# A six-stage transformer kernel on one core: the second attention's tables loaded a layer ahead, the last layer's first routing moved into the attention's last tile, and the attention's loop written out

## The reference

```
x = x + 0.5 * _L0_ffn_ref(_layernorm(x), ...)    # 4 experts, top 1, 128 -> 512 -> 128, gelu
x = x + _L0_attn_ref(_layernorm(x), ...)
x = x + 0.5 * _L0_ffn_ref(_layernorm(x), ...)
x = x + 0.5 * _L1_ffn_ref(_layernorm(x), ...)    # 32 experts of width 64, top 4
x = x + _L1_attn_ref(_layernorm(x), ...)         # 16 heads of 8, RoPE, softmax over 512 keys
x = x + 0.5 * _L1_ffn_ref(_layernorm(x), ...)
```

```
sel_logits = einsum('nd,ed->ne', xt, expert_sel); gates = sigmoid(sel_logits)
sel_val, sel_idx = top_k(gates, 4)               # gate_full: 0 outside the four
scores = relu(einsum('nd,edf->nef', xt, keys)) * gate_full[:, :, None]
out = einsum('nef,efv->nv', scores, values)

q, k, v = split(x @ w_qkv);  q, k = rope(q), rope(k)
attn = softmax(q k^T * 8 ** -0.5);  out = (attn v) @ w_proj + b_proj
```

## Time and profile before

| | us |
|---|---|
| median of three runs | 2547.51 |
| lowest, highest | 2541.93, 2551.03 |
| the profiled execution | 2552.19 |
| its span (first to last instruction) | 2550.4 |
| PE busy | 2252.5 (88%) |
| DVE busy | 1999.4 (78%) |
| ACT busy | 1298.6 (51%) |
| POOL busy | 962.2 (38%) |
| chain that ended last: PE, issue, DVE, DMA, ACT | 59%, 12%, 11%, 7%, 6% |

### The profile page before, as it was taken

The page is one execution under the profiler, slowest core; times in us unless marked ns, Lnnn a source line. Parts: engine busy times, 40 slices in busy tenths (PEclk is TensorE's granted clock), DMA queues, the critical chain, the costliest instruction groups (busy, mean ns, idle before and its releaser), DMA issues.

```text
span 2550.4 us, 39117 instructions
## 1 busy us (share of the span) xinstructions
PE 2252.5 (88%) x11234; PEld 1572.7 (62%) x11234; DVE 1999.4 (78%) x4669; ACT 1298.6 (51%) x1907; POOL 962.2 (38%) x868
## 2 busy tenths in 40 slices
PE   4399476749949999986999999999999998999999
PEld 3377355537737777764555555555555555777777
DVE  6588577748848999975888888888888885888887
ACT  1088232218824444442666666666666665444444
POOL 6600566420047777762122111112111202565654
PEclk9999655659969999996999999999999999999999
DMA  7243111024348888871111211111111113889886
GB/s 176 74 155 128 42 31 35 22 95 133 112 104 182 172 186 171 185 166 51 59 59 63 69 62 55 61 55 58 58 54 59 54 54 84 181 174 187 174 186 152
DMA packets 141318, 266.47 MB, mean 104 GB/s; under 512 B 19347, under 2 KB 22422, under 8 KB 140950
## 3 DMA queue, kind: packets, MB, share of 16 engines
q1 hardware_dynamic: 132790, 247.99, 39.7%
q0 software_dynamic: 8416, 17.25, 2.6%
HBM read 213.26 MB, written 54.31 MB: 105 GB/s over the span
## 4 chain that ended last, share of the span: by engine, by line
PE 59%; issue 12%; DVE 11%; DMA 7%; ACT 6%; SPq 3%; POOL 1%; POOLq 0%; DVEq 0%; ACTq 0%
PE ps L1960 10%; PE ps L1984 9%; PE ps L1971 8%; PE ps L1679 7%; PE ps L1681 7%; PE ps L1680 7%; DMA gate_rows<-gates_dram 4%; DVE m L1369 2%; ACT g L854 2%; PE ps L1693 1%; ACT g_hi L827 1%; PE ps L1686 1%; PE ps L1706 1%; DVE g_lo L1051 1%; DVE xnT_hl L1051 1%
## 5 line engine op out<-in xcount | busy, mean ns | idle before, releaser
L1533 DVE TENSOR_REDUCE shift<-ps 128x1 fp32r<-128x512 f32 x1024 | 664.2, 685 | 157.7 <-PE ps L1960 139.7
L978 ACT ACTIVATE prob<-ps 128x1024 f32<-128x1024 f32 x512 | 509.8, 1025 | 361.7 <-PE ps L1971 354.9
L827 ACT ACTIVATE hi<-m 128x512 fp32r<-128x512 f32 x512 | 318.8, 631 | 424.0 <-DVE m L1369 423.9
L679 POOL TENSOR_TENSOR lo<-m,hi 128x512 fp32r<-128x512 f32 x256 | 342.5, 1340 | 306.2 <-ACT hi L827 305.7
L1960 PE MATMUL ps<-k_pad,q_st 128*128 128x512 f32 x1024 | 401.7, 434 | 19.7 <-DVE shift L1533 12.9
L1369 DVE SCALAR_TENSOR_TENSOR m<-ps,gate_rows 128x512 f32<-128x512 f32 x512 | 335.0, 680 | 90.8 <-PE ps L1681 51.9
L1960 PEld LDWEIGHTS ps<-k_pad,q_st 128*128 128x128 f32 x1024 | 179.4, 190 | 263.7 <-DVE shift L1533 229.7
L1971 PE MATMUL ps<-q_sh,k_pad 128*128 128x512 f32 x1024 | 329.8, 404 | 0.0
L1984 PE MATMUL ps<-prob,v_cols 128*32 128x512 f32 x2048 | 272.7, 605 | 1.2 <-ACT o_raw L827 0.8
L1051 DVE TENSOR_TENSOR lo<-m,hi 128x512 fp32r<-128x512 f32 x256 | 209.8, 819 | 16.7 <-ACT hi L827 0.2
L1679 PE MATMUL ps<-hi,vals_hl 128*128 128x512 f32 x512 | 209.9, 410 | 0.7 <-DVE lo L1051 0.5
(11 more groups left out here) (215 smaller groups left out, 3997.1 us busy)
## 6 DMA issues: line engine op xcount, KB each, us to landing
gate_rows<-gates_dram SPq DMA_DIRECT2D x256, 512.0 KB, 6.4
w_blk<-w_dram SPq DMA_DIRECT2D x38, 514.5 KB, 3.6
q_st<-q_dram SPq DMA_DIRECT2D x64, 256.0 KB, 2.6
k_pad<-k_dram SPq DMA_DIRECT2D x256, 50.0 KB
k_dram<-qk_hl SPq DMA_DIRECT2D x48, 256.0 KB
q_dram<-qk_hl SPq DMA_DIRECT2D x48, 256.0 KB
x_blk<-sorted_x SPq DMA_DIRECT2D x38, 256.0 KB, 3.4
sorted_y<-yb_rows SPq DMA_DIRECT2D x38, 256.0 KB, 2.0
```

Source lines behind the costliest of these rows:

```text
L679: pool.tensor_tensor(m["lo"][:, s], m["m32"][:, s], m["hi"][:, s].bitcast(F32), ALU.subtract).then_inc(sig(ph, "lo_pool"), 1)
L827: return act.activation(o, i, ACT.Copy)
L978: act.activation(prob[:, h % HP, 2 * half:2 * half + 2, :], ps[:, b0:b0 + 2, :], ACT.Exp, scale=SCALE).then_inc(sig(ph, "prob"), 1)
L1533: dve.tensor_reduce(shift[:, g % 2, b, c:c + 1], wide(PASS1 + b % 2), AXX, ALU.max, negate=True).then_inc(sig(ph, "qmax"), 1)
```

## The change

It has four parts.

1. **Memory and loads.** The seven tables of the attention get memory of their own. SP loads all six of them that come from DRAM right behind the gate rows of phase 3's tile 0, `w_o` among them; `consts` therefore counts to 11 for all users. `v_cols0` moves down, so that the first 32 KB of the overlay hold nothing that tile 15's second half needs except three heads of `k_pad`. DVE splits the weights at fb 6 of the last feed-forward tile, not 10. POOL adds `bias(0)` behind the barrier.
2. **First heads.** In tile 0 of the attention SP loads a group's queries ahead of its keys.
3. **Last tile.** The routing of tile 16 moves to steps 0 to 10 of attention tile 15, through bank `MISC`; its sigmoid is made of ACT's exponential and, on DVE, an addition and a reciprocal. SP loads tile 16's gate rows once `st` shows step 7 of tile 15. `normalise(5, TILES + 1)` goes to step 12.
4. **Loop.** In phase 4 `over_tiles` writes all 16 `body` calls out. SP keeps its loop.

```diff
@@ over_tiles
             head(t0, 0)
+            if ph == 4:
+                for t in range(TILES):
+                    body(t, t % 2, t < TILES - 1)
+                return
             with eng.Fori(t0 // 2, t0 // 2 + PAIRS - 1) as pair:
@@ SyncE
             gates(0, 0, first=True)
+            sp.dma_start(stage_l[:], views["staged_late"][1][0]).then_inc(w_in, 16)
+            for dst, src in ((cos_t[:], const["cos"]), (sin_t[:], const["sin"]), (w_v[:], views["w_v"]),
+                             (w_o[:], views["w_o"]), (out_b1[:], views["out_b1"].partition_broadcast(P))):
+                sp.dma_start(dst, src).then_inc(consts, 16)
             gates(1, 1, first=True)
...
-            sp.wait_ge(sig(3, "m"), (TILES - 1) * FB1)
-            sp.dma_start(stage_l[:], views["staged_late"][1][0]).then_inc(w_in, 16)
...
+            def load_group(t, g, again):
+
+                if again:
+                    load_keys(t, g, again)
+                    load_queries(t, g, again)
+                else:
+                    pass_wait(sp, sig(4, "k_zero"), g + 1)
+                    load_queries(t, g, again)
+                    load_keys(t, g, again)
...
+            sp.wait_ge(sig(4, "st"), (TILES - 1) * 2 * HEADS + HEADS)
             gates(TILES, 0)
@@ GpSimd
                     rope_low(0, 0, 1)
-                    pool.wait_ge(consts, 16 * 10)
-                    bias(0)
...
                         last.then_inc(sig(4, "zeroed"), 1)
+                        pool.wait_ge(consts, 16 * 11)
+                        bias(t)
@@ ScalarE, attention step
+                    if h == 4 and not more:
+                        transposed(5, TILES, 0, MISC)
+                    if h == 6 and not more:
+                        act.wait_ge(sig(5, "logit"), TILES + 1)
+                        act.activation(ffn1_mem["sig"][:], ffn1_mem["logit"][:], ACT.Exp, scale=-1.0)\
+                           .then_inc(sig(5, "sigm"), 1)
                     exps(t, h, 1)
-                    if h == 12 and not more:
-                        transposed(5, TILES, 0)
+                    if h == 10 and not more:
+                        gateT(5, TILES, MISC)
@@ VectorE
-                    if fb == 10:
+                    if fb == 6:
                         attention1_weights()
...
+                    if by_exp:
+                        once.step(dve.tensor_scalar(ffn1_mem["sig"][:], ffn1_mem["sig"][:], 1.0, None, ALU.add))
+                        once.settle()
+                        once.step(dve.reciprocal(ffn1_mem["sig"][:], ffn1_mem["sig"][:]))
+                        once.settle()
...
-                    if not more and h == 11:
+                    if not more and h == 0:
                         dve.wait_ge(sig(ph, "xn"), TILES)
                         normalise(5, TILES)
-                    if not more and h == 13:
+                    if not more and h == 6:
+                        top(5, TILES, 1)
+                    if not more and h == 7:
                         x_low(5, TILES, 0)
-                    if not more and h in (14, 15):
-                        top(5, TILES, h - 14)
+                        top(5, TILES, 2, by_exp=True)
+                    if not more and h == 12:
+                        normalise(5, TILES + 1)
@@ TensorE, attention step
                     if h == 11:
 
+                        if not more:
+                            pe.wait_ge(sig(5, "gateT"), TILES + 1)
                         shifted(t, 3, p)
...
-                    if h == 12 and not more:
-                        transpose_in(5, TILES, TR)
-                    if h == 13 and not more:
-                        route(5, TILES, router1[:], E1)
+                    if h == 3 and not more:
+                        bank_read("qsh_sb", g4 + 2)
+                        transpose_in(5, TILES, MISC)
+                    if h == 4 and not more:
+                        pe.wait_ge(sig(5, "x_hi"), TILES + 1)
+                        route(5, TILES, router1[:], E1, MISC)
+                    if h == 10 and not more:
+                        bank_read("x_done", t * 4)
+                        gateT(5, TILES, MISC)
```

67 lines of the change are left out of this document (29 added, 38 removed).

## The result

| | before | after |
|---|---|---|
| median of four runs, us | 2549.27 | 2524.05 |
| lowest, highest | 2541.93, 2551.51 | 2522.84, 2526.30 |
| the profiled execution | 2552.19 | 2523.10 |
| its span | 2550.4 | 2521.3 |

The changed kernel takes 0.9907 of the time before, with a 95% interval of 0.9894 to 0.9921: 25.2 us less by the medians, where 23.0 were forecast. The four places that follow go through the program in its own order, each with rows from the profile of the changed kernel.

The account below looks back on a forecast made before the run. PE was taken as the bound, so only its stops could be won. Start 7.8, tables -0.5, loop 9.3 and tile 15 with the way into phase 5 6.4 sum to 23.0 us: 2547.5 to 2524.5, range 2514 to 2538.

Parts of the forecast that it names:

- The loop: Second attention, phase 4: six jumps back cost PE 1.56 us each; straight-line code gains 9.3 us.
- Start: End of phase 3 to first scores: earlier m 2.9, clock 2.3, bias 1.3, queries first 1.3; gain 7.8 us.
- Table loads: Phase 3, between tile 0's gate rows and tile 1's gates: six loads lose 0.5 us, bounds 0 and 4.6.
- Tile 15, steps 0 to 10: Attention's last tile: the routing added there costs 4.0 us, bounds 1.5 and 7.1.
- Behind step 11: Tile 15's end into phase 5: removed stalls and route gain 3.3 us, PE's wait behind gate rows 4.4.
- Rival 5: More gained than counted: tile 15 costs 1.5, sigmoid and statistics give another microsecond or two; 2520 us, chance 0.06.
- Clock at phase 5's start: Phase 5's first 17 matmuls take half of 5.50 us without the wait; gain 2.7 us, bounds 0 and 2.7.
- best case: Whole kernel, every bound at its best: 8.4 + 9.3 + 8.9 = 26.6 us gained.
- worst case: Whole kernel, every bound at its worst: 2.9 - 4.6 + 9.3 + 0.6 = 8.2 us gained.
- Rival 1: Waits change place: clock low at both borders, queries first brings nothing, tile 15's burst costs 7.1; 2533.9 us, chance 0.17.
- Rival 3: Attention: instructions arrive late in long straight code, 43.7 us over 14 tiles; 2568 us, chance 0.05.
- Rivals 2 and 4: 2: tile 1's gate rows 4.6 us late, 2528.6, chance 0.06; 4: loop not the cost, 2533.8, chance 0.03.

Follow-up runs that it names:

- e1: Changed kernel with the second attention back in the pair loop on all engines; 2536.75 us, ratio 0.9958.
- e12: Changed kernel with the second attention's pair loop back on DVE alone, straight-line code on PE, ACT and POOL; 2538.14 us, ratio 0.9958.
- e11: Changed kernel with the second attention's pair loop back on PE, ACT and POOL, DVE alone in straight-line code; 2528.95 us, ratio 0.9930.
- e4: Changed kernel with the six tables loaded at the end of phase 3 again and the weights split at fb 10; 2527.67 us, ratio 0.9914.
- E10: Changed kernel with POOL's low part of tile 0 at fb 10 and tile 15's last routing work at steps 12 to 14; 2521.94 us, ratio 0.9900.
- e3: Changed kernel with the last tile's routing late again, at steps 11 to 15 and behind the last output; 2535.03 us, ratio 0.9944.
- the control: The changed kernel measured again, unaltered; 2525.71 us, ratio 0.9910.
- e9: Changed kernel with both expert phases in straight-line code too; 2534.21 us, ratio 0.9945.

## Why the prediction was right, and where it was not

The forecast of 23.0 us and 2524.5 against 2524.05 measured is closer than its terms deserve.

- **The loop, 9.3 us: right** in place, size and mechanism. In the profile the fifteen pairs together lost 9.3 us, e1 and e12 bring 9.2 and 9.4 back, and e11 shows that DVE's jump is all of it. The idle time of rows 7 was the right evidence: it named the engine. The rule that a compare-and-branch takes some 108 ns (the Trainium skill, Advanced Engine Details and Errata, Control Flow Timing) does not describe this cost: it is 2.4 us a time on DVE in e12 and 2.3 in rows 7.
- **Start, 7.8 us: too large.** That 7.76 us had gone at the first score product of the first profile flatters it; 2.26 of them had gone before the gates of tile 15, and e4 with its late loads is as early there (1112.69 us against 1112.63). Counted from those gates it is 5.5 and 5.1 us in the two profiles of the changed kernel, and 2.7 in the median of the eight with the same code there. Two steps failed. One is the clock: I took 2.3 us for it, the upper bound, because a shorter stall might not cost it. It fell around the stall of 3.40 us in all nine profiles. The other is the split of the weights at fb 6, which I put at 0: with it POOL's norm takes 0.5 us longer and PE's stand at fb 9 is 1.83 to 3.13 us where it was 1.29 to 1.55. Behind that stand the clock fell in seven of eleven profiles, and in the six of them with the stall of 3.40 us nearly all of the shorter stall's gain was gone at yT. `m` 2.9 us earlier came true with 2.64 (4.90 less the 2.26), the stall of 3.4 us with 3.40, the bias with 1.2 for 1.3. The new order of the first loads brought 0.8 in all, about half of it by queries first, for 1.3.
- **Table loads, 0.5 us: right as far as can be told**, with 0.4 in the median of eleven profiles, inside their scatter. E10's 4.4 are near the upper bound of 4.6, but hold two falls of the clock, which that bound did not count. What was to show the term wrong, waits for gate rows near 770 us, is there in small: 0.78 us in the changed kernel, on DVE.
- **Tile 15, steps 0 to 10, 4.0 us: right.** 3.6 us in the profile, 3.8 in e3's comparison. I had them spread over steps 5 to 8; 2.6 of them lie in the one group with the burst of step 7. The reciprocal took 0.95 us, above my 0.76 from rows 9. The estimate of 1.07 from the Trainium skill, VectorE: DVE Perf Modes, first fixed hardware budget, is above the measured 0.95, so the true value lay between the two.
- **Behind step 11, 3.3 + 4.4 us: right, a little small.** The first `m` of phase 5 came 10.07 us earlier against that matmul in the first profile, and 8.45 in executions with the lower clock (30.09 against 21.64). Rival 5 had the sign of it: the sigmoid's table and DVE's statistics no longer stand ahead of the last output.
- **Clock at phase 5's start, 2.7 us: not shown as a gain of the change.** The first profile showed it (1.00 for 0.51), the control of the same program did not, and it held in four of the eleven. I had tied the fall to the wait of 4.44 us; in six profiles it began ahead of the barrier, behind short waits that my terms left out.
- **The sum.** In the first profile: 2.3 us of scatter ahead of the gates of tile 15, 5.5 at the start, 6.3 from the first to the last shift matmul (9.3 less 3.6, and 0.6 of scatter), 15.1 behind, 29.1 in all (2547.15 to 2518.09 at the last x). Of the 15.1 some 2.5 are the faster pace of phase 5, which the control doesn't show. The control's profile gives 2.8, 5.1, 5.6 and 10.9, 24.3 in all. So a start that was forecast 2.3 to 2.7 us too large was made good, in the first profile by a routing and a pace that gave more than their terms, in the control by the 2.8 us ahead of the gates, which no term covers. With the median start of the eight profiles (2.7 us) the control's 24.3 would be 21.9. That the forecast median came true to 0.5 us is luck: the control's median, of the same program, is 1.7 us higher. The best case of the prediction holds a slip too: its bounds give 8.1 at the start, not 8.4, and its worst case leaves out the 1.4 us of the weights.
- **The rivals.** Rival 1 was right on the clock at the first border and in most executions at the second, and wrong on the burst. Rival 3 was wrong for the attention, where it was placed. In the expert phases straight code costs 8.5 us by e9, though late instructions, its mechanism, are not shown as the cause. Rivals 2 and 4 fell.

## What to carry to other kernels

A jump back can cost one engine of a loop and none of the others. My reading is that it costs where that engine has no work in hand and the engine behind it no lead, which no run tests by itself; look for idle time that ends in "issue", see on which engine it is, and unroll that one. Unrolling everything is not free: where the loop showed no such idle time, it cost 8.5 us. Work moved to where its own engine has room can still slow another: the split of the weights seems to have slowed POOL. A short stall of TensorE may cost the clock as well, so the edit that ends a stall (one line on another engine's queue) can be worth more than one that halves it; and a clock gain seen in one profile should be booked only when a second profile of the same program shows it.

## What the runs showed of the hardware

- TensorE's clock about short stands is not settled by the program. With nearly the same waits of less than 1 us ahead of and at a barrier it stayed at 1.00 (2.4 GHz) in four profiles and fell to 0.5 (1.2 GHz) in seven, which cost some 3 us in six and 1.5 in one; two of the eleven, one up and one down, are the same program. About the end of stands of 1.83 to 3.13 us it fell in seven profiles of eleven, of stands of 1.29 to 1.55 us in none of three. Around a stand of 3.40 us it fell in all nine that have it; behind 0.79 us it stayed up.
- VectorE's jump back left it without instructions for 2.3 to 2.4 us on average, 2.8 at the longest; those of TensorE, ScalarE and GpSimd in the same loop cost nothing that can be seen. With VectorE looped a code queue fetched 23 packets more (78 against 55, 74 against 51).
- GpSimd's `rstd` took 1.31 us and the end of its norm 1.37 in the eleven profiles in which VectorE converts the weights meanwhile, 1.05 and 1.04 in the three in which it does so later.
- A reciprocal of 128x128 elements took 0.95 us, against 164 ns for 128x1: 6.2 ns for each further element.
- More code in straight line slowed two phases that had not suffered from their loops, by 8.5 us in 2525.71.
